# Transposed attention scores on 32-row blocks of TensorE, two key groups at a time

## The chip, the cores and the metric

The kernel runs on one core of a Trainium2 chip. The time is device time in microseconds (us) of one execution; below that stand the times of three runs and one profiled execution. The engines are TensorE (PE, with PEld for its weight loads), VectorE (DVE), ScalarE (ACT), GpSimd (POOL) and SyncE (SP, which only issues DMAs here).

## The reference

Two layers work on x of shape (16, 128, 256), sixteen independent batch elements of 128 tokens. Each layer has a gated cross-attention on a context of 128 rows with 64 features, and a gated feed-forward part; both take the layer norm of x.

```python
# attention, layer L: G key groups of width d (4 x 16 in layer 0, 8 x 8 in layer 1), 4 query heads per group
q = layernorm(x)                                   # split into (group, head, d)
scores = einsum('bghsd,bgtd->bghst', q, k) / sqrt(d)
out = einsum('bghst,bgtd->bghsd', softmax(scores), v)
x = x + tanh(g) * (out @ Wc.T + bc)                # layer 0; layer 1 adds out itself
# feed-forward, layer 0: silu(x @ w_gate) * (x @ w_up), 2 of every 4 kept, @ w_down
# feed-forward, layer 1: router over 8 experts, the best 2, plus a shared expert
```

## The kernel before, in words

Each batch element of a layer ("half", numbered n) passes four stages: attention_1, attention_2, ffn_1 and ffn_2. `rounds` overlaps them: in each slot four halves are in flight, one per stage, and eight slots make one round `body(p)`, with 4 batch elements for layer 0 and then the same 4 for layer 1. There are four rounds. Each engine runs a generator of each stage, and `alternate` merges the four by the table PLACE: a `yield k` puts what follows at place PLACE[(stage, layer)][k] of the slot. The order on every engine is thus written out by hand and fixed; an engine works it off in order and waits on semaphores.

attention_1 transposes the queries of one batch element (bank QK), copies them to `qt`, multiplies them with all keys in query-major form (L679) and takes the row maxima on DVE (L946); the maxima go into the query tile. attention_2 transposes the query tile again (`turn` at L693 to L696), ACT copies it to `qt` (`a_mt`, `a_mt2`), and then the transposed scores are made, one key group g at a time: keys down, 4 x 128 queries across, a bank of 512 columns. In `qt` and in the key tiles each key group has a block of BLK = 32 rows. Of these the low d rows hold rounded keys, further rows their remainders, and one row is the one-hot row through which the maximum is subtracted. In the key tiles `k0a`, `k0b` (layer 0) and `k1` (layer 1) the 128 x 128 part of group g is zero outside of the 32 rows of the group. Layer 0 takes two matmuls per group (L708, L709), layer 1 one (L711).

The scores of group g go to bank PV[g % 2]. PE signals `a_s`, ACT takes the exponential into `pt[:, g, :]` (L550) and signals `a_e`, and PE may write the bank again for group g + 2. The semaphores count in eighths, step = 8 // G. After the last group follow the products with the values on 32 columns each (L720), the division, the output projection (layer 0) and the addition to x.

The places in a slot around the scores: in layer 1 (stage attention_2) the groups 0 to 7 stand at 6, 6, 19, 24, 24, 29, 33, 37 and the value products at 46; in layer 0 the groups 0 to 3 stand at 8, 14, 26, 27 and the value products at 48. The transposes of the next attention_1 stand at 28 in layer 1, the transposes of ffn_1's norm at 21 (layer 1) or 16 (layer 0), its gate or router matmuls at 30 or 32 and the shared expert at 35. On ACT the copies for ffn_2 and ffn_1 (`ht_hi`, `at_hi`) stand at 22 and at 20 or 23, the copies of `qt` of attention_1 at 28, and each exponential at the place of its group.

Of the kernel before, what the change touches and what calls it, by code (L numbers as in the profile page):

```python
# [31 lines left out]
def flamingo_block(nc, x, ctx_kv, ctx_t, g_x, g_f, wc_t, bc, w_up, w_down, gate_w_t, gate_b, w13, w2, out):  # L32
# [8 lines left out]
    BLK = 32  # L41
# [12 lines left out]
    with ctx:  # L54
        def sb(name, shape, dt=F32):
            return ctx.enter_context(nc.sbuf_tensor(name, shape, dt))

        def sem(name):
            return ctx.enter_context(nc.semaphore(name))
# [31 lines left out]
        k0a = [sb(f"k0a_{s}", [P, G0, T], F32R) for s in range(2)]  # L91
        k0b = [sb(f"k0b_{s}", [P, G0, T], F32R) for s in range(2)]
        k1 = [sb(f"k1_{s}", [P, G1, T], F32R) for s in range(2)]
# [10 lines left out]
        qt = [sb(f"qt{b}", [P, 2, HPG * T], F32R) for b in range(2)]  # L104
# [37 lines left out]
        QK, PV, UP, DOWN = half_bank  # L142
# [21 lines left out]
        S = {n: sem(n) for n in names}  # L164
# [6 lines left out]
        def wait(eng, name, n):  # L171

            eng.wait_ge(S[name], n + 1)

        def wait_before(eng, name, n, back=1):

            if not (isinstance(n, int) and n < back):
                eng.wait_ge(S[name], n + 1 - back)

        def wait_part(eng, name, n, k):  # L180

            eng.wait_ge(S[name], 8 * n + k)
# [70 lines left out]
        def halves_index(p, s, L):  # L253

            return 2 * NS * p + NS * L + s, NS * p + s, s % 2
# [9 lines left out]
        G = [G0, G1]  # L265
# [222 lines left out]
        def _(act):  # L488
# [45 lines left out]
            def attention_2(p, s, L):  # L534
                yield 0
                n, i, b = halves_index(p, s, L)
                yield 1

                wait(act, "a_mt_ps", n)
                if L == 0:  # L540
                    act.activation(qt[b][:, 1, :], PV[0][:, :], ACT.Copy).then_inc(S["a_mt"], 1)
                else:
                    act.activation(qt[b][:, 0, :], PV[0][:, :], ACT.Copy).then_inc(S["a_mt"], 1)
                    wait(act, "a_mt_ps2", i)
                    act.activation(qt[b][:, 1, :], PV[1][:, :], ACT.Copy).then_inc(S["a_mt2"], 1)  # L545
                step = 8 // G[L]
                for g in range(G[L]):
                    yield 2 + g * step
                    wait_part(act, "a_s", n, step * (g + 1))
                    act.activation(pt[:, g, :], PV[g % 2][:, :], ACT.Exp, scale=float(HD[L]) ** -0.5)\  # L550
                       .then_inc(S["a_e"], step)
                yield 10
                wait(act, "a_pv", n)
                act.activation(ot[:, 0, :], PV[0][:, :], ACT.Copy).then_inc(S["a_ot"], 1)
                if L == 1:
                    wait(act, "a_pv2", i)
                    act.activation(ot[:, 1, :], PV[1][:, :], ACT.Copy).then_inc(S["a_ot2"], 1)
                yield 12
                if L == 0:
                    wait(act, "a_onT", i)  # L560
                    act.activation(ao_hi[:, :, :], PV[0][:, 0:D].rearrange("p (k t) -> p k t", k=KT), ACT.Copy)\
                       .then_inc(S["a_aohi"], 1)
# [43 lines left out]
            def ffn_2(p, s, L):  # L606
# [6 lines left out]
                else:  # L613
# [11 lines left out]
                    hidden_t(i, 2, 0, 4 * P)  # L625

            rounds(act, (attention_1, attention_2, ffn_1, ffn_2), round_ffn_0_weights)


        @block.tensor  # L630
        def _(pe):
# [3 lines left out]
            def product(o, a_hi, a_lo, w_hi, w_lo, first, last, free=False):  # L635

                pe.matmul(o, a_hi, w_hi, start=first, stop=False, skip_group_check=free)  # L637
                if w_lo is not None:
                    pe.matmul(o, a_hi, w_lo, start=False, stop=False, skip_group_check=free)  # L639
                return pe.matmul(o, a_lo, w_hi, start=False, stop=last, skip_group_check=free)  # L640

            def turn(o, src, count):

                for k in range(count):
                    last = pe.transpose(o[:, P * k:P * (k + 1)], src(k), ident[:, :])  # L645
                return last
# [36 lines left out]
            def attention_2(p, s, L):  # L683
                yield 0
                n, i, b = halves_index(p, s, L)
                tiles = G[L] // 4
                step = 8 // G[L]

                wait_before(pe, "a_out", n)
                wait_part(pe, "a_r", n, 8)  # L690
                if L == 0:
                    wait(pe, "a_q_hi2", n)
                    turn(PV[0], lambda j: q0b[:, j].rearrange("p g b -> p (g b)"), HPG).then_inc(S["a_mt_ps"], 1)  # L693
                else:
                    turn(PV[0], lambda j: q1[:, j, 0:4].rearrange("p g b -> p (g b)"), HPG).then_inc(S["a_mt_ps"], 1)
                    turn(PV[1], lambda j: q1[:, j, 4:8].rearrange("p g b -> p (g b)"), HPG).then_inc(S["a_mt_ps2"], 1)  # L696

                for g in range(G[L]):
                    yield 2 + g * step
                    if g == 0:  # L700
                        wait(pe, "a_mt", n)
                        if L == 1:
                            wait(pe, "a_mt2", i)
                    if g >= 2:
                        wait_part(pe, "a_e", n, step * (g - 1))
                    o = PV[g % 2][:, :]
                    if L == 0:
                        pe.matmul(o, k0a[b][:, g, :], qt[b][:, 0, :], start=True, stop=False)  # L708
                        last = pe.matmul(o, k0b[b][:, g, :], qt[b][:, 1, :], start=False, stop=True)  # L709
                    else:  # L710
                        last = pe.matmul(o, k1[b][:, g, :], qt[b][:, g // 4, :], start=True, stop=True)  # L711
                    last.then_inc(S["a_s"], step)
                yield 10

                wait(pe, "v0_done" if L == 0 else "v1_done", i)
                vv = v0[b] if L == 0 else v1[s]
                wait_part(pe, "a_e", n, 8)
                for t in range(tiles):
                    for g in range(4):
                        last = pe.matmul(PV[t][BLK * g:BLK * (g + 1), :], vv[:, 4 * t + g, :], pt[:, 4 * t + g, :],  # L720
                                         start=True, stop=True)
                    last.then_inc(S["a_pv" if t == 0 else "a_pv2"], 1)
                yield 11
                wait(pe, "a_ot", n)
                turn(PV[1] if L == 0 else PV[0], lambda j: ot[:, 0, P * j:P * (j + 1)], HPG).then_inc(S["a_otT"], 1)
                if L == 1:
                    wait(pe, "a_ot2", i)
                    turn(PV[1], lambda j: ot[:, 1, P * j:P * (j + 1)], HPG).then_inc(S["a_otT2"], 1)
                else:
                    yield 12  # L730
                    wait(pe, "a_on", n)
                    turn(PV[0], lambda k: on[:, P * k:P * (k + 1)], KT).then_inc(S["a_onT"], 1)
                    yield 13
                    wait(pe, "a_aohi", i)
                    wait(pe, "a_aolo", i)
                    if isinstance(p, int) and p == 0 and s == 0:
                        pe.wait_ge(S["c_hi"], 2)
                        pe.wait_ge(S["c_lo"], 2)
                    for k in range(KT):
                        last = product(PV[1][:, 0:D], ao_hi[:, k, :], ao_lo[:, k, :], wc_hi[:, k, :], wc_lo[:, k, :],  # L740
                                       k == 0, k == KT - 1)
                    last.then_inc(S["a_proj"], 1)
# [59 lines left out]
            def ffn_2(p, s, L):  # L802
# [34 lines left out]
                else:  # L837
# [34 lines left out]
                    down(range(8, 12), w2_r, None, NT1 - 1, NT1 - 2).then_inc(S["f_y"], 1)  # L872

            rounds(pe, (attention_1, attention_2, ffn_1, ffn_2))


# [263 lines left out]
```

## Time and profile before

| | us |
|---|---|
| median of 3 runs | 762.33 |
| lowest, highest | 761.54, 769.18 |
| span of the profiled execution | 763.7 |
| PE busy | 642.4 |
| DVE busy | 477.8 |
| ACT busy | 464.6 |
| POOL busy | 235.0 |

The span goes from the first to the last instruction of the profiled execution. Busy times are shares of that span in which the engine had an instruction running; ends of matmuls are modelled. The engines run at the same time, so the busy times are not to be added.

### The profile page before, as it was taken

Reading aid. Unit: us, or ns where it says so; the run is one execution under the profiler, and the core shown is the slowest. Engines: PE = TensorE matmul, PEld = TensorE weight load, DVE = VectorE, ACT = ScalarE, POOL = GpSimd, SP = SyncE. Lnnn points to the kernel's source line nnn. Section 1 sums busy time; section 2 is a strip of 40 time slices with the busy share of each in tenths; the row PEclk is TensorE's granted clock in tenths of the full one; section 3 lists DMA queues with packets and bytes.
Section 4 is the critical chain, followed back from the end, with each engine's and each line's share of the span. In section 5 each row is a group of like instructions: output and inputs, shape, how many; then the busy total and the mean of one; then the engine's idle time right before and its main releaser. Section 6 shows DMA issues by size and latency. Waiting matters only on the chain.

```text
span 763.7 us, 12585 instructions
## 1 busy us (share of the span) xinstructions
PE 642.4 (84%) x3792; PEld 492.2 (64%) x3792; DVE 477.8 (63%) x1153; ACT 464.6 (61%) x851; POOL 235.0 (31%) x497
## 2 busy tenths in 40 slices
PE   0455888899999988898999988898999988899866
PEld 0233567677677767676777766676777767677655
DVE  3422777856556777766556777766556777867433
ACT  2422656667875656675876656675875655677642
POOL 5111443321331433421332433421331433331110
PEclk9996799989999999999999999999999999999979
DMA  8371040000000000000000000000000000000000
GB/s 254 99 224 47 15 91 1 6 5 6 22 22 22 20 8 3 4 7 9 22 21 22 21 6 4 3 7 8 22 21 13 8 1 1 5 7 7 1 8 15
DMA packets 21840, 20.79 MB, mean 27 GB/s; under 512 B 7584, under 2 KB 20816, under 8 KB 20816
## 3 DMA queue, kind: packets, MB, share of 16 engines
q1 hardware_dynamic: 19328, 12.75, 6.6%
q0 software_dynamic: 1888, 4.87, 2.2%
q10 hardware_dynamic: 560, 2.36, 0.9%
q8 instruction: 36, 0.59, 0.3%
q14 instruction: 28, 0.23, 0.1%
HBM read 12.28 MB, written 5.24 MB: 23 GB/s over the span
## 4 chain that ended last, share of the span: by engine, by line
PE 55%; DVE 14%; issue 10%; ACT 7%; POOL 5%; SPq 5%; DMA 3%; DVEq 0%; POOLq 0%; ACTq 0%
PE bank L637 14%; PE bank L640 12%; PE bank L645 9%; PE bank L720 6%; PE bank L639 5%; PE bank L679 4%; PE bank L711 3%; SPq L314 2%; DVE q L946 2%; ACT L593 2%; ACT L591 2%; DMA kd<-down_lo 1%; PE bank L708 1%; SPq L303 1%; DVE f_stat L914 1%
## 5 line engine op out<-in xcount | busy, mean ns | idle before, releaser
L946 DVE TENSOR_REDUCE q<-bank 128x4 f32<-128x512 f32 x128 | 84.4, 688 | 53.4 <-PE bank L679 51.8
L550 ACT ACTIVATE pt<-bank 128x512 f32<-128x512 f32 x192 | 108.6, 606 | 15.1 <-PE bank L711 9.1
L637 PE MATMUL bank<-w_r,at_hi 128*128 128x352 f32 x288 | 101.4, 353 | 5.2 <-ACT work L619 2.3
L640 PE MATMUL bank<-w_r,at_lo 128*128 128x352 f32 x288 | 95.2, 332 | 0.0
L987 DVE SCALAR_TENSOR_TENSOR work<-bank,cw,work 128x176 f32<-128x176 f32 x128 | 45.2, 395 | 55.5 <-ACT work L619 47.3
L637 PEld LDWEIGHTS bank<-w_r,at_hi 128*128 128x128 f32 x288 | 56.6, 196 | 24.6 <-ACT work L619 12.9
L711 PE MATMUL bank<-qt,k 128*128 128x512 f32 x128 | 56.6, 477 | 17.8 <-ACT qt L545 10.8
L1075 DVE TENSOR_TENSOR ht_lo<-bank,ht_hi 128x512 fp32r<-128x512 f32 (+1 forms) x96 | 57.9, 618 | 16.5 <-ACT ht_hi L602 13.8
L637 PE MATMUL bank<-up_hi,at_hi 128*128 128x512 f32 x128 | 53.9, 421 | 15.5 <-DVE at_lo L1028 15.0
L602 ACT ACTIVATE ht_hi<-bank 128x512 fp32r<-128x512 f32 (+1 forms) x96 | 50.5, 545 | 26.2 <-PE bank L645 26.1
L946 DVE TENSOR_REDUCE q0b<-bank 128x4 f32<-128x512 f32 x64 | 42.1, 687 | 29.3 <-PE bank L679 29.3
L645 PE MATMUL bank<-ident,work 128*128 128x128 f32 x336 | 52.2, 280 | 7.1 <-DVE y L1106 2.6
L640 PEld LDWEIGHTS bank<-w_r,at_lo 128*128 128x128 f32 x288 | 56.6, 197 | 2.0
L434 POOL TENSOR_TENSOR work<-work,keep 128x512 f32<-128x512 f32 x32 | 37.7, 1179 | 62.8 <-DVE keep L1014 62.8
L639 PE MATMUL bank<-up_lo,at_hi 128*128 128x512 f32 x128 | 52.1, 407 | 0.0
L645 PEld LDWEIGHTS bank<-ident,work 128*128 128x128 f32 x336 | 39.0, 142 | 20.4 <-DVE work L987 6.5
L640 PE MATMUL bank<-up_hi,at_lo 128*128 128x512 f32 x128 | 52.0, 406 | 0.0
L637 PE MATMUL bank<-w_r,ht_hi 128*128 128x256 f32 x208 | 51.1, 286 | 0.0
L679 PE MATMUL bank<-k,qt 128*128 128x512 f32 x128 | 49.1, 425 | 2.2 <-DVE q L946 2.2
L423 POOL TENSOR_SCALAR lose<-lose 128x256 bf16<-128x256 bf16 x32 | 15.6, 488 | 112.9 <-DVE lose L1003 111.6
L720 PE MATMUL bank<-pt,v 128*32 128x512 f32 x384 | 49.2, 615 | 0.9 <-ACT pt L550 0.8
L640 PE MATMUL bank<-w_r,ht_lo 128*128 128x256 f32 x208 | 49.9, 281 | 0.0
(159 smaller groups left out, 1615.4 us busy)
## 6 DMA issues: line engine op xcount, KB each, us to landing
w_r<-in_w POOLq DMA_DIRECT2D x1, 3168.0 KB, 14.7
x<-in_x SPq DMA_DIRECT2D x16, 128.0 KB, 2.1
work<-in_w_up ACTq DMA_DIRECT2D x2, 1024.0 KB, 6.6
k<-kd SPq DMA_DIRECT2D x128, 12.0 KB
out<-y SPq DMA_DIRECT2D x16, 128.0 KB, 1.8
w_r<-in_w POOLq DMA_DIRECT2D x1, 1536.0 KB, 6.6
kd0a<-down_hi SPq DMA_DIRECT2D x8, 128.0 KB, 5.6
k0a<-kd0a SPq DMA_DIRECT2D x64, 16.0 KB, 1.6
```

The source lines that it names most:

```text
L550: act.activation(pt[:, g, :], PV[g % 2][:, :], ACT.Exp, scale=float(HD[L]) ** -0.5)\
L602: act.activation(ht_hi[:, 4 * t:4 * t + cols // P, :], DOWN[b][:, 0:cols].rearrange("p (k t) -> p k t", t=P), ACT.Copy)\
L637: pe.matmul(o, a_hi, w_hi, start=first, stop=False, skip_group_check=free)
L639: pe.matmul(o, a_hi, w_lo, start=False, stop=False, skip_group_check=free)
L640: return pe.matmul(o, a_lo, w_hi, start=False, stop=last, skip_group_check=free)
L645: last = pe.transpose(o[:, P * k:P * (k + 1)], src(k), ident[:, :])
L679: pe.matmul(QK[(1 + m) % 2][:, :], qt[b][:, t, P * j:P * (j + 1)], k_[:, 4 * t:4 * t + 4, :].rearrange("p g t -> p (g t)"), start=True, st ...
L711: last = pe.matmul(o, k1[b][:, g, :], qt[b][:, g // 4, :], start=True, stop=True)
L720: last = pe.matmul(PV[t][BLK * g:BLK * (g + 1), :], vv[:, 4 * t + g, :], pt[:, 4 * t + g, :], start=True, stop=True)
L946: dve.tensor_reduce(o, QK[(1 + m) % 2][:, :].rearrange("p (g t) -> p g t", t=T), AX.X, ALU.max, negate=True).then_inc(S["a_r"], step)
L987: last = dve.scalar_tensor_tensor(out=hid[b][:, EI * e:EI * (e + 1)], in0=o[:, EI * k:EI * (k + 1)], scalar=cw[b][:, e:e + 1], in1=sg[b][: ...
L1075: dve.tensor_tensor(ht_lo[:, r, :], DOWN[b][:, 0:cols].rearrange("p (k t) -> p k t", t=P), ht_hi[:, r, :].bitcast(F32), ALU.subtract).then ...
```

## The change

PE now makes the transposed scores of two groups together. Each matmul contracts over the 32 rows of its own group alone (a slice r of the key tile and of `qt`), so the two matmuls of a pair use two different blocks of 32 rows of the array, and they write to the two banks PV[0] and PV[1]. A pair needs both banks free: PE waits for the exponentials of both groups of the pair before. `a_s` counts once for a pair, and ACT waits for the pair. The places are those of the even groups: 6, 19, 24 and 33 in layer 1, 8 and 26 in layer 0. The exponentials keep theirs.

```diff
@@ attention_2 on ACT
                 for g in range(G[L]):
                     yield 2 + g * step
-                    wait_part(act, "a_s", n, step * (g + 1))
+                    wait_part(act, "a_s", n, 2 * step * (g // 2 + 1))
                     act.activation(pt[:, g, :], PV[g % 2][:, :], ACT.Exp, scale=float(HD[L]) ** -0.5)\
                        .then_inc(S["a_e"], step)
@@ attention_2 on PE
-                for g in range(G[L]):
+                for g in range(0, G[L], 2):
                     yield 2 + g * step
                     if g == 0:
                         wait(pe, "a_mt", n)
                         if L == 1:
                             wait(pe, "a_mt2", i)
-                    if g >= 2:
-                        wait_part(pe, "a_e", n, step * (g - 1))
-                    o = PV[g % 2][:, :]
+                    else:
+                        wait_part(pe, "a_e", n, step * g)
+                    rows = [slice(BLK * (h % 4), BLK * (h % 4) + BLK) for h in (g, g + 1)]
                     if L == 0:
-                        pe.matmul(o, k0a[b][:, g, :], qt[b][:, 0, :], start=True, stop=False)
-                        last = pe.matmul(o, k0b[b][:, g, :], qt[b][:, 1, :], start=False, stop=True)
+                        for h, r in zip((g, g + 1), rows):
+                            pe.matmul(PV[h % 2][:, :], k0a[b][r, h, :], qt[b][r, 0, :], start=True, stop=False)
+                        for h, r in zip((g, g + 1), rows):
+                            last = pe.matmul(PV[h % 2][:, :], k0b[b][r, h, :], qt[b][r, 1, :], start=False, stop=True)
                     else:
-                        last = pe.matmul(o, k1[b][:, g, :], qt[b][:, g // 4, :], start=True, stop=True)
-                    last.then_inc(S["a_s"], step)
+                        for h, r in zip((g, g + 1), rows):
+                            last = pe.matmul(PV[h % 2][:, :], k1[b][r, h, :], qt[b][r, h // 4, :], start=True,
+                                             stop=True)
+                    last.then_inc(S["a_s"], 2 * step)
```

## Rows read from the trace of the kernel before

**Rows 1.** The page, busy time by engine, and shares of the last chain.

```profile
PE 642.4 (84%) x3792; PEld 492.2 (64%) x3792; DVE 477.8 (63%) x1153; ACT 464.6 (61%) x851; POOL 235.0 (31%) x497
...
PE 55%; DVE 14%; issue 10%; ACT 7%; POOL 5%; SPq 5%; DMA 3%; DVEq 0%; POOLq 0%; ACTq 0%
```

**Rows 2.** Windows: span, busy us (instructions) of PE, PEld, DVE, ACT, POOL, clock, DMA.

```profile
295.00:466.00 171.00, 154.70 (x952) 119.73 (x951) 115.91 (x285) 113.49 (x211) 56.30 (x117) 0.99 0.05 13
```

**Rows 3.** The page, costliest groups: busy, mean ns, idle before and what ended it.

```profile
L550 ACT ACTIVATE pt<-bank 128x512 f32<-128x512 f32 x192 | 108.6, 606 | 15.1 <-PE bank L711 9.1
...
L711 PE MATMUL bank<-qt,k 128*128 128x512 f32 x128 | 56.6, 477 | 17.8 <-ACT qt L545 10.8
```

**Rows 4.** Timeline of PE in slot A: start us, us, engine, line, operation, count.

```profile
305.33 0.40 PE L679 MATMUL bank<-k,qt 128*128 128x512 f32 x1
305.66 0.64 PE L720 MATMUL bank<-pt,v 128*32 128x512 f32 x4
...
306.97 0.61 PE L720 MATMUL bank<-pt,v 128*32 128x512 f32 x4
307.51 0.51 PE L679 MATMUL bank<-k,qt 128*128 128x512 f32 x1
...
310.09 0.40 PE L640 MATMUL bank<-up_hi,at_lo 128*128 128x512 f32 x1
310.33 0.40 PE L637 MATMUL bank<-up_hi,at_hi 128*128 128x512 f32 x1
```

**Rows 5.** Timeline of PE and ACT, slot A, 298.5 to 301.8 us.

```profile
298.62 0.71 PE L711 MATMUL bank<-qt,k 128*128 128x512 f32 x2
...
299.40 0.58 ACT L550 ACTIVATE pt<-bank 128x512 f32<-128x512 f32 x1
...
300.03 0.50 PE L711 MATMUL bank<-qt,k 128*128 128x512 f32 x1 [0.70 <-ACT pt L550]
...
300.49 1.06 PE L645 MATMUL bank<-ident,q 128*128 128x128 f32 x8
...
300.62 1.10 ACT L550 ACTIVATE pt<-bank 128x512 f32<-128x512 f32 x2
...
301.31 0.47 PE L711 MATMUL bank<-qt,k 128*128 128x512 f32 x1
...
301.62 0.39 PE L637 MATMUL bank<-up_hi,at_hi 128*128 128x512 f32 x1
```

**Rows 6.** Timeline of PE and ACT, slot B, 320.8 to 324.1 us.

```profile
320.87 0.80 PE L711 MATMUL bank<-qt,k 128*128 128x512 f32 x2
...
321.74 1.12 ACT L550 ACTIVATE pt<-bank 128x512 f32<-128x512 f32 x2
...
322.00 1.07 PE L645 MATMUL bank<-ident,q 128*128 128x128 f32 x8 [0.34 <-POOL q L398]
...
322.69 0.65 ACT L529 ACTIVATE qt<-bank 128x512 fp32r<-128x512 f32 x1
...
323.14 0.17 PE L637 MATMUL bank<-gate_hi,at_hi 128*128 128x8 f32 x1
...
323.65 0.67 ACT L550 ACTIVATE pt<-bank 128x512 f32<-128x512 f32 x1
323.73 0.48 PE L711 MATMUL bank<-qt,k 128*128 128x512 f32 x1
...
324.04 0.33 PE L637 MATMUL bank<-w_r,at_hi 128*128 128x352 f32 x1
```

**Rows 7.** Timeline of PE and ACT, slot E, 386.9 to 389.3 us.

```profile
387.05 1.09 ACT L550 ACTIVATE pt<-bank 128x512 f32<-128x512 f32 x2
...
387.91 0.48 PE L708 MATMUL bank<-qt,k0a 128*128 128x512 f32 x1
```

**Rows 8.** Windows in the last round's slot A, columns as in rows 2.

```profile
644.20:647.50 3.30, 3.30 (x12) 2.71 (x11) 0.88 (x2) 2.14 (x5) 1.16 (x1) 0.50 0.02 5
```

**Rows 9.** Timeline of PE at the start of slot D.

```profile
360.63 0.73 PE L645 MATMUL bank<-ident,q 128*128 128x128 f32 x3 [2.46 <-issue]
```

## Prediction

> **What bounds the kernel now.** I read the page first: TensorE (PE) is busy 84% of the span and holds 55% of the chain that ended last; no other engine holds more than 14% [rows 1]. The windows then say where. After some 85 us of loading, one round of the loop takes 171 us for eight slots, and PE is busy in 154.7 us of them, so only 16 us of a round are PE's own waits [rows 2]. A slot takes 19 to 25 us. Call the slots of a round A to D (starting near 295, 316, 335 and 359 us), in which attention_2 works on layer 1, and E to H, in which it works on layer 0. PE works in program order, so what matters is where in a slot it waits, and whether the work behind the wait is dense. In the timeline each slot begins with a thin stretch (norms, transposes, the scores and their exponentials) and is dense from the first gate matmul on. The changed instructions are in the thin stretch. There ACT, not PE, decides: 192 exponentials of 0.61 us each, and the score matmuls had PE idle 17.8 us before them, 10.8 of it for the copy of qt [rows 3].
>
> **What a matmul and a change of shape cost.** Full matmuls of 512 columns follow one another every 0.23 us, their weight loads hidden (310.09 to 310.33) [rows 4]. If the load could not run ahead, the step is 0.31 (301.31 to 301.62) [rows 5]: an exposed load is 0.09. The trace has no matmul on a block of 32 rows. The nearest is the value product L720, on blocks of 32 columns. The full matmul at 305.33 should have been followed after 0.23; the first narrow one starts after 0.33: entering costs 0.10. Its 16 instructions go in four passes of four column blocks that start together, from 305.66 to 306.97, so 0.44 a pass; the last streams until about 307.40, and the next full load starts at 307.51: leaving costs 0.11, and its load is exposed, 0.09 more [rows 4]. I take these prices for row blocks, since that is the only change of array shape in the trace. The lower end is zero (a shape change cannot make a stream shorter than its columns); the upper end is that the two streams do not overlap, which adds 0.23 for each pair. Four column blocks do start together, so I take full overlap.
>
> The trace shows the array emptying at a change of shape, by the 0.10 and 0.11 above. The Trainium skill, TensorEngine Tiling (Array Packing), section Key Properties, says the same: changing the tiling mode drains TensorE. Its section PSUM Bottleneck says that tiling speeds up TensorE and not the evacuation of PSUM, which speaks against this change: the exponentials are that evacuation. In TensorE: Matmul & The Clock Gate, Part 3, a pack of row tiles takes one matmul plus 4 ns a tile, with no price for the change of shape; by that the sum below would be some 6 us smaller, and no run here shows it yet.
>
> **Part 1: fewer streams.** 64 layer-1 pairs (128 matmuls of L711) and 64 rounds of pairs of layer 0 each save one stream of 0.23: 128 x 0.235 = 30 us of PE time at the very most. A lone layer-1 pair in dense work costs 0.10 + 0.09 + 0.23 + 0.11 + 0.09 = 0.62, against 0.46 for two plain matmuls: +0.16. A layer-0 block (four matmuls, two rounds) costs 0.85 against 0.92. Where PE waits before the pair anyway, the entry costs nothing and the two come out equal. So the array itself gives nothing back.
>
> **Part 2: the waits.** Before, group g needs only exponential g-2, so PE fills one bank while ACT empties the other. Now a pair needs both banks empty: the pair (2,3) waits for exponential 1, the pair (4,5) for 3, the pair (6,7) for 5. What queues behind these waits on PE is the rest of the slot. With the order in PLACE, the pair (4,5) follows the pair (2,3) with at most two transposes between.
>
> Slot A [rows 5]. Group 4 starts at 300.03, when exponential 2 (299.40, 0.58) ends. Exponential 3 starts at 300.62, behind at_hi and ht_hi on ACT, and ends at 301.22. The pair (4,5) then starts at 301.27; PE has nothing in between, since the eight transposes of q (300.49) stand behind it. It streams until 301.59, leaves at 301.70, the transposes take 0.82 + 0.11, and the gate matmuls start near 302.63 instead of 301.62: +1.0. The pair (6,7) stands in dense work: +0.16. Slot A: +1.15.
>
> Slot B [rows 6]. Exponential 3 starts at 321.74, so it ends at 322.34 and the pair (4,5) starts at 322.40, where groups 3 and 4 went at 320.87 and 321.18. The transposes begin at 322.85 instead of 322.00, and the router matmuls at 323.76 instead of 323.14. On ACT exponential 4 now starts when the pair ends, 322.90; the two copies of qt need the transposes and start at 323.50 and 323.98 (now 322.69 and 323.17); exponential 5 starts at 324.46 instead of 323.65 and ends at 325.06. The pair (6,7), placed ahead of the shared expert, waits for it until 325.11, while PE is through with the router at 324.35. The shared expert starts at 325.54 instead of 324.04: +1.5. Group 7's own matmul behind it is gone (-0.23), but the third row-maximum matmul waits for the reduction of the first, which moved by the whole 1.5. Slot B: +1.5.
>
> Slot C repeats B, with the same steps at 340 to 343 us: +1.5. In D no transposes of q stand between, and PE has idle time ahead of the transposes of q0a: +0.8.
>
> Layer 0, slot E [rows 7]. The second pair waits for exponential 1 (387.05 + 0.49 + 0.60 = 388.14) instead of starting at 387.91, and both of its exponentials come 0.3 later, as do q0a's copy and transposes: +0.3. In F to H the work behind it (the norm's transposes, at_lo) comes later than the pair, so neither the wait nor the saved streams show: 0.
>
> After these stretches PE is dense to the end of the slot, and the next slot's first transposes follow PE's last matmul, so A, B and C count in full: 4.15 x 4 rounds = 16.6 us. D and E have loop turn and pipeline fill around them, and I count half: 1.1 x 4 / 2 = 2.2. Sum 18.8: the profiled 763.7 would become 782.5. The profiled span is 1.4 above the median of the runs (762.3), so I forecast 781 us, 2.4% slower. DVE, POOL and the loads get no other work; SP's reload of k waits for the same last count of a_s as before.
>
> **Rivals.** (a) A change of row blocks is free. The waits stay: A loses 0.55 of its 1.15, B and C about 0.4 of 1.5: (0.6 + 1.1 + 1.1) x 4 + 2 = 13 us, 775 us. For it: nothing in these rows; against it: [rows 4]. (The Trainium skill's pack of row tiles, cited above, would give this case.) (b) The two streams do not overlap, each on its own bank but through the same array: 0.23 more for the pairs (4,5) and (6,7) in A to C, 5.6 us, and about 2 in D and E: 789 us. Against it: the column blocks overlap. (c) The clock falls more often. In 644.20 to 647.50 us the granted clock is 0.50, its lower level (1.2 GHz), in the slot like A of the last round [rows 8], and transposes are slow as well after PE has stood 2.46 us until 360.63 [rows 9]. At half the clock such a stretch of 3.3 us does the work of 1.65. In A PE would stand from 299.2 to 301.27, longer than anywhere in that slot now. A fall in each of the 12 slots A to C adds 12 x 1.6 = 19 us: 800 us. (d) Little or nothing: the lateness is taken up by PE's later waits (16 us a round) and the change of shape is cheap. Half of 13 us: 769 us, inside 1%. Against it: the waits lie ahead of the dense work, not behind. (e) Faster: PE is the limit everywhere and the doubled wait falls behind other work. It decides if ACT has both exponentials done when PE comes to the next pair, which in A to C needs 1.1 us of other work between the pairs (2,3) and (4,5). There is 0.2 to 0.3. Then up to 30 us of streams would be gained, and with the idle stretches some half of it: 748 us.
>
> **How the numbers follow.** My forecast, 0.52; (a) 0.14; (b) 0.06; (c) 0.08; (d) 0.12; (e) 0.08. A difference of 1%, 7.6 us, is about what the runs can tell from none: they spread by as much. The cases (a) to (c) and the forecast are slower by over 1%: 0.80. Within 1%: 0.12. Faster: 0.08. The range for 8 in 10 leaves out (e), half of (d) and the end of (c): 768 to 799 us.
>
> **What would show it.** In the changed profile, two L711 matmuls should start within some 10 ns of each other (overlap) or 0.23 apart (rival b). The next full weight load should come about 0.34 after their streams began. The pair (4,5) should name ACT's exponential as what ended PE's wait, in A about 2 us after the pair before it. PE's idle before L711 should rise from 17.8 to over 35 us while its busy time falls by up to 30. A slot B or C should be 1.5 us longer, A 1.1, E to H nearly unchanged. I would be wrong if ACT took the exponentials in another place of its order, if the later waits of DVE or ACT took up the lateness, or if the change of row block cost much more than that of a column block.

## The result, and the profile after

The changed kernel takes 845.3 us (median of 4 runs, 842.3 to 846.1) against 761.9 for the kernel before in the same session: a ratio of 1.107, 95% interval 1.101 to 1.112. The forecast was slower, 781 us with a range to 799; the direction held, and the loss of 83 us is more than four times the 19 that I had worked out. The profiled execution spans 843.8 us, 80 more than the 763.7 before.

From the page after: the busy times that answer to [rows 1], the strip of the granted clock, the chain, and the groups that answer to [rows 3] (L714 is the old L711).

```profile
PE 691.6 (82%) x3792; PEld 507.5 (60%) x3792; DVE 477.1 (57%) x1153; ACT 470.6 (56%) x851; POOL 234.3 (28%) x497
...
PEclk9967888788999898689899888788899998888979
...
PE 63%; ACT 13%; issue 8%; DVE 7%; SPq 4%; DMA 3%; POOL 2%; DVEq 0%; ACTq 0%; POOLq 0%
...
L550 ACT ACTIVATE pt<-bank 128x512 f32<-128x512 f32 x192 | 107.3, 597 | 40.7 <-PE bank L714 29.9
...
L714 PE MATMUL bank<-qt,k 32*128 32x512 f32 x128 | 39.4, 609 | 43.0 <-ACT pt L550 31.1
```

The score matmuls are cheaper, 39.4 us busy for layer 1 instead of 56.6. Yet PE is busy 49 us more in all, with the same number of matmuls, and its idle time before the layer-1 scores went from 17.8 to 43.0 us, now mostly for the exponentials. More busy time for less work points to the clock. The granted clock of the whole span, in the view by cores, after and before:

```profile
core 0: 843.8 us, clock 0.862
```
```profile
core 0: 763.7 us, clock 0.960
```

At two levels, 1 and 0.5, a mean of 0.862 means 2 x 0.138 x 843.8 = 233 us at the lower one (1.2 GHz), against 61 us before. The windows show it by stage. The first answers to [rows 2], one round of eight slots; the next two are stretches of it at the lower clock; the last is the same round of the kernel before, between the same points:

```profile
317.61:512.01 194.40, 171.32 (x950) 126.65 (x950) 115.61 (x286) 115.34 (x212) 55.93 (x117) 0.86 0.04 11
...
320.40:327.20 6.80, 4.82 (x18) 3.71 (x16) 1.62 (x3) 4.27 (x9) 1.87 (x2) 0.50 0.01 2
344.30:357.90 13.60, 11.49 (x41) 6.66 (x45) 4.33 (x8) 6.89 (x17) 4.12 (x10) 0.50 0.03 9
```
```profile
296.40:467.20 170.80, 154.49 (x948) 119.53 (x949) 115.71 (x285) 113.49 (x212) 56.10 (x117) 0.99 0.05 13
```

This round takes 194.4 us instead of 170.8 and has about 54 us at the lower clock instead of 3. (The rounds before and behind it take 188.9 and 192.0 us instead of 170.9 and 172.4, with some 45 us at the lower clock each instead of 10 and 7.) PE is busy 17 us more in it and idle 7 us more (23.1 against 16.3). DVE, ACT and POOL have nearly the same busy time as before.

Slot A again, PE and ACT, the rows that answer to [rows 5]:

```profile
319.97 0.50 PE L714 MATMUL bank<-qt,k 32*128 32x512 f32 x2
...
321.31 0.60 ACT L602 ACTIVATE ht_hi<-bank 128x512 fp32r<-128x512 f32 x1
321.79 0.61 ACT L550 ACTIVATE pt<-bank 128x512 f32<-128x512 f32 x1
322.45 0.79 PE L714 MATMUL bank<-qt,k 32*128 32x512 f32 x2 [1.98 <-ACT pt L550]
323.17 1.97 PE L645 MATMUL bank<-ident,q 128*128 128x128 f32 x8
...
324.79 0.78 PE L637 MATMUL bank<-up_hi,at_hi 128*128 128x512 f32 x1
```

The wait is the one that was forecast: the pair (4,5) stands 1.98 us for exponential 3, which stands behind at_hi and ht_hi. But the clock falls at 320.4 (the window from 320.40), and what follows runs at half of it: the eight transposes take 1.97 us instead of 1.06. This fall comes before the wait, since the pair (2,3) ends at 320.47. The 4.8 us up to it, from the transposes of q on, stand beside the same stretch of the kernel before:

```profile
315.60:320.40 4.80, 2.95 (x18) 1.88 (x18) 4.04 (x12) 3.91 (x7) 3.86 (x9) 1.00 0.01 2
```
```profile
294.40:299.20 4.80, 2.99 (x19) 2.16 (x18) 4.05 (x12) 3.88 (x7) 3.89 (x9) 1.00 0.01 2
```

PE is as busy in both and does the same work, but for the four score matmuls, which are over 32 rows in the first. Behind it the clock falls to 0.50; in the kernel before it stays at 1.00.

### The profile page after: what moved, and what is told of

Read it like the earlier page. It is cut to its first block, busy times and chain, and to the rows that moved or that the text cites. A ratio compares the mean times of both kernels' runs of the same rounds, so it can differ in the third digit from the quotient of the medians.

```text
span 843.8 us, 12504 instructions
## 1 busy us (share of the span) xinstructions
PE 691.6 (82%) x3792; PEld 507.5 (60%) x3792; DVE 477.1 (57%) x1153; ACT 470.6 (56%) x851; POOL 234.3 (28%) x497
## 4 chain that ended last, share of the span: by engine, by line
PE 63%; ACT 13%; issue 8%; DVE 7%; SPq 4%; DMA 3%; POOL 2%; DVEq 0%; ACTq 0%; POOLq 0%
PE bank L637 15%; PE bank L640 13%; PE bank L645 11%; PE bank L724 7%; PE bank L639 6%; PE bank L679 6%; ACT pt L550 5%; PE bank L714 3%; SPq L314 2%; DMA kd<-down_lo 1%; PE bank L709 1%; ACT L550 1%; SPq L303 1%; ACT L593 1%; ACT L591 1%
## 5 line engine op out<-in xcount | busy, mean ns | idle before, releaser
L637 PE MATMUL bank<-w_r,at_hi 128*128 128x352 f32 x288 | 108.6, 378 | 5.1 <-ACT work L619 2.2
L640 PE MATMUL bank<-w_r,at_lo 128*128 128x352 f32 x288 | 99.6, 347 | 0.0
L714 PE MATMUL bank<-qt,k 32*128 32x512 f32 x128 | 39.4, 609 | 43.0 <-ACT pt L550 31.1
L637 PE MATMUL bank<-up_hi,at_hi 128*128 128x512 f32 x128 | 60.5, 473 | 16.3 <-DVE at_lo L1032 16.0
L724 PE MATMUL bank<-pt,v 128*32 128x512 f32 x384 | 64.2, 784 | 0.0
L640 PEld LDWEIGHTS bank<-w_r,at_lo 128*128 128x128 f32 x288 | 59.9, 208 | 0.7
L639 PE MATMUL bank<-up_lo,at_hi 128*128 128x512 f32 x128 | 57.4, 448 | 0.0
L640 PE MATMUL bank<-up_hi,at_lo 128*128 128x512 f32 x128 | 56.3, 440 | 0.0
L679 PE MATMUL bank<-k,qt 128*128 128x512 f32 x128 | 53.1, 473 | 2.9 <-DVE q L950 2.9
L645 PE MATMUL bank<-ident,q 128*128 128x128 f32 x256 | 47.9, 349 | 7.2 <-issue 4.7
```

Of the source, the lines that this page charges most:

```text
L679: pe.matmul(QK[(1 + m) % 2][:, :], qt[b][:, t, P * j:P * (j + 1)], k_[:, 4 * t:4 * t + 4, :].rearrange("p g t -> p (g t)"), start=True, st ...
L714: last = pe.matmul(PV[h % 2][:, :], k1[b][r, h, :], qt[b][r, h // 4, :], start=True, stop=True)
```

## Experiments

Twelve kernels, in three batches, each batch beside the kernel before on one chip. Two theories stood at first: **W**, the added waits make PE idle, and the idle time makes the clock fall; **S**, matmuls over 32 rows themselves do. In the second batch S was split into **A**, the array's missing work counts, and **D**, the emptying at each change of shape does.

The row of a round (eight slots from an A on) in each kernel, columns as in rows 2, stands with each experiment. Time at the lower clock in a round is twice (1 - clock) of its length; with two decimals of the clock that is good to about 2 us.

**e1: pairs over all rows.** The changed kernel with
```diff
-                    rows = [slice(BLK * (h % 4), BLK * (h % 4) + BLK) for h in (g, g + 1)]
+                    rows = [slice(0, P) for h in (g, g + 1)]
```


> The changed kernel, but each matmul of a pair contracts over all 128 rows again: the order and the doubled wait stay, the change of array shape and the overlap of the streams go. Theory W (the wait makes PE idle in the thin stretch, and the idle time makes the clock fall): nearly as slow as the changed kernel, 835 to 855 us, with some 230 us at the lower clock. Theory S (matmuls on 32 rows count for little with whatever grants the clock, so the shape makes it fall): near my forecast for the waits alone, 780 to 790 us, with under 100 us at the lower clock.

Measured: 815.1 us, ratio 1.064 (1.058 to 1.070), clock 0.937.
```profile
307.00:491.00 184.00, 157.77 (x951) 123.55 (x950) 115.61 (x285) 114.27 (x212) 55.96 (x116) 0.96 0.04 12
```
Between the two theories' numbers, so neither holds alone. The waits of the pairs and the serial streams, with the clock falls that they bring, cost 51 us; the 32-row shape adds 30.

**e2: single groups over 32 rows.** The kernel before, old order and old waits, with
```diff
-                        pe.matmul(o, k0a[b][:, g, :], qt[b][:, 0, :], start=True, stop=False)
+                        r = slice(BLK * (g % 4), BLK * (g % 4) + BLK)   # likewise for k0b and k1
+                        pe.matmul(o, k0a[b][r, g, :], qt[b][r, 0, :], start=True, stop=False)
```


> The kernel before, in its old order and with its old waits, but each score matmul contracts over its own 32 rows. Theory W: 765 to 780 us (some 0.3 us of shape changes at each of up to 192 places, part of them where PE waits anyway), clock as in the kernel before. Theory S: the clock falls in every slot and the time is above 810 us.

Measured: 836.0 us, ratio 1.092 (1.086 to 1.097), clock 0.875.
```profile
314.90:506.10 191.20, 176.46 (x950) 127.41 (x949) 115.67 (x285) 115.51 (x212) 56.06 (x117) 0.88 0.04 12
```
No wait was added here, PE is idle for 14.7 us of the round where it was 16.3, and yet 46 us of it are at the lower clock. Theory W can't do this. The shape alone costs 72 us, in clock and in changes of shape together.

**e3: filler.** The changed kernel with
```diff
                     last.then_inc(S["a_s"], 2 * step)
+                    fill = {(0, 0): 6, (1, 0): 4, (1, 2): 8}.get((L, g), 0)
+                    for _ in range(fill):        # k0a in layer 0
+                        pe.matmul(QK[0][:, :], k1[b][:, g, :], qt[b][:, 0, :], start=True, stop=True)
```


> The changed kernel with extra full matmuls of 512 columns into the idle bank QK[0], whose results nobody reads: 6 behind the first pair of layer 0, 4 behind the first and 8 behind the second pair of layer 1, where PE would wait. They add PE work of 0.9 to 1.9 us at each place. Theory W: the clock stays up and, although PE has more to do, the time falls to 780 to 800 us. Theory S: the clock still falls at the pairs; no better than 835 us. If neither idle time nor shape sets the clock, the time rises above 845 us.

Measured: 831.8 us, ratio 1.084 (1.077 to 1.091), clock 0.940. The second row is slot A alone.
```profile
310.20:500.10 189.90, 173.15 (x1024) 130.21 (x1022) 115.67 (x285) 115.07 (x212) 56.13 (x117) 0.96 0.04 12
...
310.20:332.80 22.60, 21.77 (x129) 15.64 (x127) 16.03 (x37) 14.49 (x26) 6.66 (x15) 1.00 0.02 5
```
288 unused matmuls (12 in each of 16 halves, 6 in each of the other 16) of 0.235 are 68 us of added streams, and the kernel is 13 us faster than the changed one, since the clock is up for longer. Both theories' numbers were missed. In slot A, where the clock is 1.00 throughout, the slot takes 22.6 us where it took 21.3, against the +1.15 of my step. The pair (4,5) starts 4.85 us behind the slot's first pair (311.47 and 316.32), where my step has 4.84 (301.27, and 296.43 in the trace before). Exponential 3 ends at 316.27, and the filler would let the pair start at the same 316.32, so it does not add to the wait. The step is right once the clock holds. The pair (6,7), in dense work at full clock, shows the prices too:

```profile
318.86 0.40 PE L640 MATMUL bank<-up_hi,at_lo 128*128 128x512 f32 x1
319.19 0.49 PE L714 MATMUL bank<-qt,k 32*128 32x512 f32 x2
319.61 0.73 PE L679 MATMUL bank<-k,qt 128*128 128x512 f32 x2
```

**e4: layer 0 alone.** The pairs on 32 rows for L == 0; layer 1 keeps the old loop.
```diff
+                two = 2 if L == 0 else 1
-                for g in range(G[L]):
+                for g in range(0, G[L], two):      # for L == 1 the old matmul, waits and counts
```


> The change in layer 0 alone (pairs at places 8 and 26); layer 1 as in the kernel before. My prediction's steps: 0 to +3 us. Theory W: idle time in layer 0's slots grows only where the second group's matmuls were taken out between the first pair and the norm, so 765 to 785 us. Theory S: as many falls of the clock as in the changed kernel's slots E to H, about 20 us more than before, 780 to 790 us.

Measured: 783.4 us, ratio 1.024 (1.017 to 1.030), clock 0.928.
```profile
304.00:479.10 175.10, 156.95 (x950) 121.22 (x949) 115.59 (x285) 113.87 (x211) 56.02 (x116) 0.95 0.05 13
```
20 us, where my steps give 0 to 3. A round has some 17 us at the lower clock, 14 more than before; at up to half a microsecond lost for each, that is 7 us, more than the 4.3 by which the round grew. The time lies in the ranges of both theories and does not part them. Where the clock is at 1.00 my steps hold: slots F and G take 40.9 us together (417.3 to 458.2), as before (405.4 to 446.3), and one slot E takes 20.8 (570.0 to 590.8) instead of 20.5.

**e5: full matmul first, then 32 rows.** e2 with each group's matmuls made twice.
```diff
+                    for r in (slice(0, P), slice(BLK * (g % 4), BLK * (g % 4) + BLK)):
+                        ...                       # the matmuls of e2 with this r, into the same bank
```


> The kernel before, in its old order, with each group's matmuls made twice into the same bank: first over all 128 rows, then over the group's 32 rows, which stand. It has all of the old streams, all shape changes of single groups on 32 rows, and 192 streams more. The single groups on 32 rows alone took 836 us. Theory A (what is missing for the clock is the columns times rows that the array works through): the clock is up again, and the time is below that, 785 to 815 us, in spite of the added work. Theory D (emptying the array at each change of shape is what makes the clock fall): clock and time as there or worse, 835 us and more.

Measured: 868.0 us, ratio 1.139 (1.130 to 1.148), clock 0.927. Below: the round of this kernel, then its longest stretch at full clock, 152 us from inside slot E to the end of C, and slot D behind it; then the like stretches of E to C in e2 and in the kernel before.
```profile
330.10:531.30 201.20, 192.06 (x1014) 133.97 (x1013) 115.68 (x285) 116.86 (x211) 56.08 (x117) 0.93 0.04 11
...
252.00:404.00 152.00, 144.46 (x816) 104.01 (x816) 99.65 (x239) 89.72 (x160) 45.33 (x88) 1.00 0.04 10
404.00:428.00 24.00, 23.53 (x66) 12.66 (x65) 3.24 (x10) 12.12 (x23) 4.43 (x13) 0.50 0.02 6
```
```profile
231.00:394.00 163.00, 149.89 (x817) 108.92 (x818) 103.04 (x250) 97.22 (x177) 49.55 (x100) 0.90 0.04 11
```
```profile
211.00:360.00 149.00, 134.58 (x835) 104.53 (x833) 105.50 (x258) 96.39 (x178) 49.57 (x100) 1.00 0.04 12
```
The time is what I had put to theory D, and the clock speaks for A in part. With every change of shape of e2 still there, and the old streams back, it is at 1.00 for 152 us, where e2 has 0.90. But at the loop's turn, where PE stands for 2.67 us, it falls and stays at 0.50 for 24 us of slot D, with PE busy in 23.5 of them; so the round has 28 us at the lower clock, against 46 in e2 and 3 before. Neither theory had said so, and no run explains it. The time missed A's numbers also because I had priced the added work too low: the added streams are 256 and not 192, at 0.235 each 60 us. I take it, without a run that shows it, that the changes of shape (0.10, 0.11 and two exposed loads) are paid in full where PE no longer waits around them.

**e6: single groups over 64 rows.**
```diff
-                    r = slice(BLK * (g % 4), BLK * (g % 4) + BLK)
+                    r = slice(2 * BLK * (g % 4 // 2), 2 * BLK * (g % 4 // 2) + 2 * BLK)
```


> As the kernel with single groups on 32 rows (836 us), but contracting over the 64 rows of two blocks, of which one is zero in the key tile. The shape changes are the same in number. Theory A: between the kernel before and that one, 780 to 815 us. Theory D: as that one, 825 to 845 us.

Measured: 827.9 us, ratio 1.087 (1.079 to 1.094), clock 0.902.
```profile
306.40:496.40 190.00, 176.52 (x952) 128.03 (x950) 115.69 (x285) 115.38 (x212) 56.11 (x117) 0.89 0.04 12
```
Between 32 and 128 rows in clock (0.875, 0.902, 0.960), nearer to 32; in time it lies with theory D and outside A's 780 to 815. It does not tell the two apart.

**e7: dense streams.** The kernel before, with this behind PE's last work:
```diff
+            for rows, count in ((full, 80), (row32, 120), (full, 80), (row64, 120), (full, 80), (pair, 120)):
+                for m in range(count):
+                    r = rows[m % len(rows)]        # slices of 128, 32 or 64 rows; pair: two blocks of 32 (definitions left out)
+                    pe.matmul(QK[r.start // BLK][:, :], k1[1][r, 4 + r.start // BLK, :], qt[1][r, 1, :], start=True, stop=True)
```


> The kernel before with six dense streams of 512-column matmuls behind its last work, results unused: 80 over 128 rows, 120 over 32, 80 over 128, 120 over 64, 80 over 128, and 120 in alternation on two blocks of 32 rows into two banks. No waits inside. Theory A: the granted clock falls to the lower level during the streams over 32 rows although PE never waits, and comes back in the streams over 128; each matmul over 32 rows then takes 0.43 us. Theory D: there is no change of shape inside a stream, so the clock stays up in all of them and a matmul takes 0.21 to 0.24 us.

Measured once (905.3 us, which says only that streams were added): windows inside the six streams, in order, with the start of the second ahead of its main part, and two lines of PE's timeline in the second and the sixth.
```profile
755.00:773.00 18.00, 18.00 (x78) 14.47 (x78) 0.48 (x1) 0.00 (x0) 0.00 (x0) 1.00 0.02 7
773.60:778.10 4.50, 4.50 (x20) 3.57 (x20) 0.00 (x0) 0.00 (x0) 0.00 (x0) 1.00 0.01 4
779.00:820.00 41.00, 41.00 (x98) 31.34 (x97) 0.00 (x0) 0.00 (x0) 0.00 (x0) 0.50 0.00 0
823.00:841.00 18.00, 18.00 (x73) 14.46 (x73) 0.00 (x0) 0.00 (x0) 0.00 (x0) 0.92 0.00 1
843.00:870.00 27.00, 27.00 (x118) 21.43 (x116) 0.00 (x0) 0.00 (x0) 0.00 (x0) 1.00 0.00 1
871.00:888.00 17.00, 17.00 (x74) 13.77 (x74) 0.00 (x0) 0.00 (x0) 0.00 (x0) 1.00 0.00 0
889.00:903.40 14.40, 14.27 (x121) 11.08 (x120) 0.00 (x0) 0.00 (x0) 0.00 (x0) 1.00 0.00 0
```
```profile
799.45 1.05 PE L882 MATMUL bank<-qt,k 32*128 32x512 f32 x2
...
894.74 0.86 PE L882 MATMUL bank<-qt,k 32*128 32x512 f32 x6
```
This is the clearest of the twelve. PE is busy without a gap in all six, nothing waits, no shape changes inside a stream. Over 32 rows on one block the clock is at 1.00 for the first 4.5 us, with a matmul every 0.23 us, and then at 0.50, its lower level, for the whole window of 41 us, with a matmul every 0.43 (the two from 799.45 take 1.05, the last of them 0.62); it comes back at 825.9, in the stream over 128 rows. Over 64 rows it stays at 1.00. So does it with two blocks of 32 side by side, at least for these 14 us: six such matmuls in 0.86 us are three overlapping pairs, each pair the 0.23 of one stream. Theory D's numbers fail; A's hold. The key tile is zero outside of a group's 32 rows, so over 64 and over 128 rows the added rows held zero weights, and the clock stayed up all the same: what went with it here is the rows that a matmul takes in, not the nonzero weights in them.

**e8: the first pair only.** Groups 0 and 1 as a 32-row pair, which needs no exponential; the others one by one over 128 rows.
```diff
-                for g in range(0, G[L], 2):
+                for g in (0, *range(2, G[L])):       # both groups, and 32 rows, at g == 0 only
```


> Only the first two groups of each half go as a pair on 32-row blocks, which needs no wait for an exponential; the others go one by one over 128 rows as in the kernel before. 32 places of shape change instead of 96. By my steps for the waits and streams: -2 to +2 us. Theory A: one of two or of four streams goes and the others count less, so some more falls: 765 to 785 us.

Measured: 774.8 us, ratio 1.018 (1.010 to 1.026), clock 0.943. No wait is added and 32 pairs of blocks are left, and it is still 12 us slower, inside theory A's 765 to 785.
```profile
297.70:474.70 177.00, 159.98 (x951) 123.71 (x950) 115.69 (x285) 114.26 (x212) 55.95 (x117) 0.94 0.05 12
```

**e9: filler in the kernel before.** Behind the last matmul of slot C:
```diff
+                    if s == 0:
+                        for _ in range(10):
+                            pe.matmul(DOWN[0][:, :], ht_hi[:, 8, :], w13_r[:, 0, 0:512], start=True, stop=True)
```


> The kernel before with 10 matmuls of 512 columns over 128 rows, results unused, behind the last matmul of each round's slot C, ahead of the 2.5 us in which PE stands at the loop's turn. If idle time is what makes the clock fall there, the falls at the start of slot D go (3.4 and 6.8 us at the lower clock in rounds 2 and 3), and the time falls by up to 1.5 us a round: 755 to 763 us. If the matmuls delay the turn instead of filling it, it rises by up to 2.3 us a round: 763 to 772 us.

Measured: 773.8 us, ratio 1.015 (1.010 to 1.021), clock 0.958. PE's timeline there:
```profile
359.30 2.49 PE L875 MATMUL bank<-w_r,ht_hi 128*128 128x512 f32 x10
362.11 0.76 PE L645 MATMUL bank<-ident,q 128*128 128x128 f32 x5 [0.32 <-issue]
365.08 0.33 PE L645 MATMUL bank<-ident,q 128*128 128x128 f32 x1 [2.21 <-issue]
```
The time is 2 us above the range for matmuls that delay the turn. The filler delays the turn of the loop and does not fill it: the 2.2 us without a matmul come behind it, inside the transposes. No way to a faster kernel, and it leaves open what idle time costs in clock there.

**e10, e11, e12: both exponentials at the pair's place.** The same edit on ACT in the changed kernel (e10), in e1 (e11) and in e3 (e12):
```diff
                 for g in range(G[L]):
-                    yield 2 + g * step
+                    yield 2 + g // 2 * 2 * step
```


> The changed kernel, with both exponentials of a pair at the pair's place on ACT: the odd ones no longer behind at_hi and ht_hi (place 20 to 23) or the copies of qt (28). The waits of the pairs (4,5) and (6,7) shrink by 0.4 to 1.0 us each. If the waits and the idle time they make carry part of the loss: 800 to 830 us. If the 32-row shape alone carries the clock's part: 825 to 840 us. If neither, 845.

> Pairs over all 128 rows (815 us) with both exponentials at the pair's place. The shape is that of the kernel before; what is left of the change is the pairing. If the waits carry its loss, 780 to 800 us; if not, 810 to 820 us.

> The changed kernel with the unused full matmuls behind the first two pairs (832 us) and both exponentials at the pair's place. The filler now takes longer than the shorter waits, so some of it delays PE, but the clock should hardly fall: 805 to 830 us, with under 90 us at the lower clock. If the filler brought the clock up only because PE was otherwise idle, nothing is gained over the kernel with exponentials at the pair alone.

Measured: e10 834.5 us, ratio 1.096 (1.088 to 1.104), clock 0.865; e11 790.6 us, 1.042 (1.034 to 1.049), clock 0.954; e12 798.0 us, 1.047 (1.041 to 1.054), clock 0.961. A round of each:
```profile
314.00:505.10 191.10, 170.26 (x950) 125.49 (x949) 115.53 (x285) 114.86 (x211) 55.95 (x117) 0.87 0.04 12
```
```profile
301.30:478.90 177.60, 154.71 (x951) 120.60 (x950) 115.67 (x285) 113.93 (x212) 56.08 (x117) 0.99 0.04 12
```
```profile
301.40:483.70 182.30, 169.86 (x1023) 129.27 (x1022) 115.58 (x285) 114.39 (x212) 56.00 (x116) 0.97 0.04 12
```
e11 against e10 is the change's shape by itself: the same order, the same short waits, and 128 rows or 32. It is 44 us, and 16 us of PE's busy time in a round, with a clock of 0.99 against 0.87. e10 and e11 lie in the ranges that I had given for the shape carrying the clock's part and for the waits carrying the pairing's loss; e12 is faster than its range. e11 shows the pairing without the clock: a round is 6.8 us longer than before at the same 0.99, and the kernel 29 us slower. Shorter waits take 24 us off e1 and 11 off the changed kernel. And e12 has the 288 unused matmuls of e3 on top of e10, 68 us of streams, in part where PE would have waited, and is 37 us faster than it: what the streams cost, the clock gives back with interest.

## Why the prediction was right and wrong

- **Shape and overlap: right.** The pairs start together (317.61, two matmuls in 0.51 us) and the next full matmul comes 0.44 later, against 0.43 from my exposed load, stream and leaving. Its weight load comes with it, at 0.44 and not at my 0.34: the sum was right, its split was not. At full clock in dense work (e3 above) the entry is 0.33 instead of 0.23, the 0.10 of [rows 4], and the next full matmul comes 0.42 later. PE's timeline after:

```profile
317.61 0.51 PE L714 MATMUL bank<-qt,k 32*128 32x512 f32 x2 [0.83 <-ACT qt L545]
318.05 0.66 PE L645 MATMUL bank<-ident,work 128*128 128x128 f32 x4
```
  Rivals (a) and (b) are out.
- **The waits: right in place, and right in size where it could be seen at full clock.** The pair (4,5) in slot A waits for exponential 3 (2 us, as forecast), and e3's slot A at clock 1.00 took 1.3 more against my 1.15. Slots B and C were not seen at full clock throughout with these waits; my +1.5 for them is open (with the shorter waits of e12 a slot B took 20.3 us at 1.00 instead of 19). Shortening the waits saved 11 us of the changed kernel and 24 with full rows (e10, e11); that these are clock and wait together, the runs do not part.
- **The clock: the step that failed.** My sum has no term for the clock; I priced it in rival (c) alone, with a chance of 0.08, as 3.3 us at the lower level in each of 12 slots, 19 us. It was about 51 us more than before in the round shown (some 35 and 39 in the two others), in layer 0's slots too. The round shown by stretches, against what my steps gave:

| slots | before us (clock) | after us (clock) | longer | my steps |
|---|---|---|---|---|
| A | 21.4 (1.00) | 24.7 (0.86) | 3.3 | 1.15 |
| B | 18.9 (1.00) | 24.8 (0.72) | 5.9 | 1.5 |
| C | 26.4 (0.96) | 31.1 (0.84) | 4.7 | 1.5 |
| D | 21.8 (0.97) | 24.5 (0.86) | 2.7 | 0.8 |
| E to H | 82.3 (1.00) | 89.3 (0.90) | 7.0 | 0.3 |

  My steps are 5.25 of the 23.6 us. The other 18.4 are, as an estimate, what the 51 us cost, 0.36 for each; half speed sets 0.5 as the most. Behind the wrong size stands a wrong reason: I took a change of shape to cost only the time in which the array empties, and took that from L720, whose four column blocks at once use all 128 rows. What a matmul over 32 rows does to the clock, no row of the trace before could show; e7 shows it, and e10 against e11 shows 44 us for the shape in this kernel, at a clock of 0.865 instead of 0.954. I should have left the range open upward. That the old kernel stood near an edge was to be seen: its clock had fallen at 644 us [rows 8] in the thin stretch of a slot A, and not in the same stretch of the other rounds.
- **"The array itself gives nothing back": too kind.** e2 shows 72 us for the shape alone and e11 against e10 44. Which path one takes from before to after matters: the pairing with full rows 51 (e1), then the shape 30; or the shape first 72, then the pairing 9. The parts overlap in the same clock falls and are not to be added.
- **Layer 0: wrong by the same step.** E to H were to lose 0.3 us a round; e4 lost 20 us in all, while its slots E, F and G at full clock lasted what I had said. With full rows the pairing itself costs time there too: in e11 E to H take 85.2 us at clock 1.00 (394.9 to 480.1) instead of 82.3.
- **The rules of the Trainium skill.** Its drain at a change of tiling mode (TensorEngine Tiling (Array Packing), Key Properties) fits the trace, at 0.1 us each way. Its section PSUM Bottleneck on the same page says that tiling does not speed up the evacuation of PSUM, and the trace agrees: 31.1 us of PE's idle time before L714 end with an exponential.

## What to carry to other kernels

Using fewer rows of the array saved nothing in the length of a stream (0.23 us over 32, 64 and 128 rows), and it can cost the clock of everything behind it, in a dense stream (e7) as in thin stretches (e2); check the granted clock of each stretch before and after, and count PE's busy time for the same instructions. Two tiles that overlap win only if their results can be evacuated without PE waiting; here a pair on the only two banks turned double buffering off. And a price read from another shape's rows (column blocks on all rows) carries the time of that shape and not its effect on the clock.

## What the runs showed of the hardware that I had not expected

- A dense stream of 512-column matmuls over 32 rows, without a gap, ran at the lower clock (0.50, 0.43 us each) for a window of 41 us, after 4.5 us at 1.00; over 64 rows, over 128, and on two blocks of 32 rows at once it ran at 1.00 (e7, the last for 14 us).
- With single groups over 64 rows in the kernel's thin stretches the clock fell more often than before (e6: 0.902 against 0.960). How much of that the missing rows do and how much the changes of shape, the runs do not part.
- The second matmul behind a change of shape, or behind a wait, starts late as well, 0.33 us after the first instead of 0.23, as if its load were exposed by 0.10. In layer 0 this is the second round of a pair. It is not a trait of 32-row blocks: e3's two full matmuls from 319.61 have it behind a pair (0.73 us for two of 0.39), the kernel before has it over 128 rows behind a wait (the second fence), and inside e7's stream on one 32-row block the matmuls follow one another every 0.23, the loads hidden.

```profile
445.08 0.50 PE L709 MATMUL bank<-qt,k0a 32*128 32x512 f32 x2
445.41 0.40 PE L711 MATMUL bank<-qt,k0b 32*128 32x512 f32 x2
```
```profile
384.95 0.50 PE L708 MATMUL bank<-qt,k0a 128*128 128x512 f32 x1
385.29 0.39 PE L709 MATMUL bank<-qt,k0b 128*128 128x512 f32 x1
```
- Ten matmuls queued ahead of the loop's turn did not cover it: the 2.2 us gap followed them (e9).
